# Two stages of a graph network stop loading key rows, and a rare tile is turned on the chip instead

## The reference

```python
src, dst = src[argsort(dst)], sorted(dst)
x = layernorm(x + gnn0(x, src, dst))
x = layernorm(x + gnn1(x, edge_index, edge_attr_32, ...))
x = layernorm(x + attention(x, edge_index, ...))          # needs x[dst] of every edge
s1 = concat(xs[:, :8], xd[:, :8]); v1 = ...               # xs = x[src], xd = x[dst]
edge_out = concat(tanh(scal), vecs * tanh(gates)) * norm
x = layernorm(x + segment_sum(edge_out, dst))             # tensor product
```

## Time and profile before

| | |
|---|---|
| median of 3 runs | 26533.92 us (26527.65 to 26547.35) |
| profiled execution | 26542.53 us, span 26540.7 us |
| busy share of the span | PE 57%, DVE 58%, POOL 59%, ACT 20% |
| attention scatter | about 12034 to 16020 us |
| tensor product | about 18390 to 26500 us |

### The profile page before, as it was taken

One profiled execution on the slowest core, in us unless ns is written; L12 is line 12 of the kernel. 1 busy time (PEld: TensorE's weight loads), 2 busy tenths in 40 slices (PEclk: granted clock), 3 DMA queues, 4 the chain that ended last, 5 costly groups with the idle time before them and its releaser, 6 DMA issues. The chain is left out here.

```text
span 26540.7 us, 456722 instructions
## 1 busy us (share of the span) xinstructions
PE 15258.6 (57%) x102440; PEld 9002.1 (34%) x102441; DVE 15401.4 (58%) x31597; ACT 5213.2 (20%) x13760; POOL 15770.5 (59%) x16798
## 2 busy tenths in 40 slices
PE   7555555566666689951000000024777777787777
PEld 5344444333333388920000000023333333333333
DVE  9666666656566644431111118985666666666666
ACT  4211111111111144410000000000222222222222
POOL 0377777677777744416777777721555555555554
PEclk9655555555555555555555555555888888888888
DMA  2466666433333345403333332212444444444444
GB/s 66 117 173 172 173 173 173 112 68 69 68 69 68 63 148 154 131 15 86 92 92 92 92 92 70 71 46 66 111 111 111 110 110 110 110 111 110 110 110 104
DMA packets 2864906, 2738.33 MB, mean 103 GB/s; under 512 B 1320271, under 2 KB 2226317, under 8 KB 2861906
## 3 DMA queue, kind: packets, MB, share of 16 engines
q1 hardware_dynamic: 2297486, 2308.45, 31.4%
q0 software_dynamic: 412544, 241.53, 6.1%
q10 hardware_dynamic: 153668, 172.93, 2.6%
HBM read 2173.30 MB, written 537.93 MB: 102 GB/s over the span
## 5 line engine op out<-in xcount | busy, mean ns | idle before, releaser
L2225 POOL DMA_INDIRECT rows_x<-x_table,index x3125 | 2974.6, 952 | 3538.4 <-DMA index<-in_src 2765.6
L742 POOL DMA_INDIRECT rows<-split_table,index x3125 | 2999.6, 960 | 1937.5 <-DMA index<-in_src 1008.2
L1624 POOL DMA_INDIRECT rows_dram<-rows,place_now x3125 | 3026.4, 968 | 1484.9 <-issue 952.3
L858 POOL DMA_INDIRECT rows<-x_table,index x3125 | 3279.8, 1050 | 1021.3 <-issue 952.1
L2339 DVE TENSOR_TENSOR second<-banks,h 128x768 f32<-128x768 f32 x2500 | 1944.8, 820 | 1597.8 <-PE banks L2494 1597.8
L1552 DVE TENSOR_REDUCE rows<-banks 128x108 f32<-128x324 f32 x1250 | 490.7, 434 | 3467.3 <-DMA rows_dram<-rows,place_now 3450.7
L1564 PE MATMUL banks<-row_pieces,hot_turned 128*128 x3125 | 394.1, 291 | 3604.6 <-DMA hot_turned<-turned_dram 3602.0
L2331 DVE TENSOR_TENSOR first<-banks,h 128x768 f32<-128x768 f32 x2500 | 1937.9, 818 | 259.3 <-issue 138.3
L550 PE MATMUL banks<-counts,low_turned 128*128 128x98 f32 x6250 | 1793.3, 435 | 80.3 <-ACT counts L538 47.3
L550 PEld LDWEIGHTS banks<-counts,low_turned 128*128 128x128 f32 x6250 | 1600.9, 314 | 205.4 <-issue 175.1
L2469 PE MATMUL banks<-u_turned,w_tensor 32*128 32x384 f32 (+1 forms) x10000 | 1565.0, 501 | 145.3 <-DVE second L2339 145.3
(11 more groups left out here) (480 smaller groups left out, 33841.6 us busy)
## 6 DMA issues: line engine op xcount, KB each, us to landing
key_row<-dst_rows SPq DMA_DIRECT2D x1250, 320.0 KB, 3.5
h<-hidden_dram SPq DMA_DIRECT2D x1250, 320.0 KB, 4.2
acc_moved<-dst_rows SPq DMA_DIRECT2D x625, 320.0 KB
src_row<-in_src_rows SPq DMA_DIRECT2D x625, 320.0 KB
hot_turned<-turned_dram SPq DMA_DIRECT2D x1250, 160.0 KB, 3.2
hot_dram<-onehot SPq DMA_DIRECT2D x625, 160.0 KB
turned_dram<-hot_turned SPq DMA_DIRECT2D x625, 160.0 KB
a_dram<-a ACTq DMA_DIRECT2D x625, 160.0 KB
```

The lines of the kernel that those rows point to most:

```text
L742: nc.gpsimd.indirect_dma_start(out=m["rows"][j][:, t * SPLIT:(t + 1) * SPLIT], out_offset=None, in_=m["split_table"], in_offset=bass.Indir ...
L858: nc.gpsimd.indirect_dma_start(out=m["rows"][j][:, t * C2:t * C2 + F], out_offset=None, in_=m["x_table"], in_offset=bass.IndirectOffsetOnA ...
L1624: nc.gpsimd.indirect_dma_start(out=m["rows_dram"], out_offset=bass.IndirectOffsetOnAxis(ap=m["place_now"][j][:, t:t + 1], axis=0), in_=m[" ...
L2225: nc.gpsimd.indirect_dma_start(out=m["rows_x"][j][:, t * F:(t + 1) * F], out_offset=None, in_=m["x_table"], in_offset=bass.IndirectOffsetO ...
```

## The change

No key row is loaded in these two stages any more. The tables `key_row` and `part_at` go. If a group has a further visit, DVE makes the straight one-hot tile (edges on partitions) from the resident keys, PE turns it by multiplying each of its five 128x128 tiles with an identity matrix, and DVE copies the five results into `turned_more`. In the scatter the keys (128x3125 floats) are loaded once at the start of the stage, DVE and PE wait for that and for the half-precision identity, and `hot_turned` gets five buffers, loaded after `owned` of the group five before instead of after a join. In the tensor product `hot_turned` keeps three buffers; the line that issued `key_row` is gone and the rest of SP's order stands.

```diff
+def turn_spare_dve(nc, dve, m, s, g, further, k, bank):
+    dve.wait_ge(s["more_owned"], ONE + further + k - 1)
+    spare_hot(nc, m, g, k).then_inc(s["spare_hot"], 1)
+    for t in range(T):
+        dve.wait_ge(s["spare_turned"], ONE + T * (further + k - 1) + t + 1)
+        nc.vector.tensor_copy(m["turned_more"][:, t * P:(t + 1) * P], bank).then_inc(s["spare_out"], 1)
+def turn_spare_pe(nc, pe, m, s, further, k, bank):
+    pe.wait_ge(s["spare_hot"], ONE + further + k)
+    for t in range(T):
+        pe.wait_ge(s["spare_out"], ONE + T * (further + k - 1) + t)
+        nc.tensor.matmul(bank, m["hot_spare"][:, t * P:(t + 1) * P], m["ident_half"][:, :], start=True, stop=True).then_inc(s["spare_turned"], 1)
+    pe.wait_ge(s["spare_out"], ONE + T * (further + k))
...
 (stage_attention_tables)
-            link(nc.vector.tensor_scalar(m["part_at"][:, :], m["starts"][:, :], m["part"][:, :], None, ALU.add))
...
 (stage_attention_scatter)
-        dve.wait_ge(s["key_in"][j], 16 * (i + 1))
         with dve.If(n > 1):
             with dve.Fori(1, n) as k:
-                dve.wait_ge(s["more_owned"], ONE + further + k - 1)
-                nc.vector.tensor_scalar(m["turned_more"][:, :], m["key_row"][j % 3][:, :], m["part_at"][:, bass.ds(k, 1)], None, ALU.is_equal
-                                        ).then_inc(s["more_turned"], 1)
+                turn_spare_dve(nc, dve, m, s, SLOTS * i + j, further, k, spare_bank)
...
+            sp.dma_start(m["keys"][:, :], m["keys_dram"]).then_inc(s["loaded"], 16)
             def load(i, j):
                 g = SLOTS * i + j
-                if not (isinstance(i, int) and g < 3):
-                    sp.wait_ge(s["joined"], ONE + g - 1)
-                sp.sem_inc(s["going_sp"], 1)
-                sp.dma_start(m["hot_turned"][j % 3][:, :], ...)
-                sp.dma_start(m["key_row"][j % 3][:, :], key_row_of(m, g, "dst_rows")).then_inc(s["key_in"][j], 16)
+                if not (isinstance(i, int) and i == 0):
+                    sp.wait_ge(s["owned"], ONE + g - SLOTS + 1)
+                sp.dma_start(m["hot_turned"][j][:, :], ...)
...
 (block.tensor)
+            pe.wait_ge(s["halved"], ONE + 1)
 (block.vector)
+            nc.vector.tensor_copy(m["ident_half"][:, :], m["ident"][:, :]).then_inc(s["halved"], 1)
+            dve.wait_ge(s["loaded"], 16)
...
 (stage_directions)
-            link(nc.vector.tensor_scalar(m["part_at"][:, :], m["starts"][:, :], m["part"][:, :], None, ALU.add))
+            link(nc.vector.tensor_copy(m["ident_half"][:, :], m["ident"][:, :]))
...
 (stage_tensor_product, sp_group)
-        sp.dma_start(m["key_row"][j % 3][:, :], key_row_of(m, g, "dst_rows")).then_inc(s["key_in"][j], 16)
 (dve_turned_further)
         with dve.If(n > 1):
             _, visits, further = half_window_of(nc, dve, m, s, SLOTS * i + j)
-            dve.wait_ge(s["key_in"][j], 16 * (i + 1))
-            turned(slice(1, 2)).then_inc(s["more_turned"], 1)
-            with dve.If(visits > 2), dve.Fori(2, visits) as k:
...
+            with dve.Fori(1, visits) as k:
+                turn_spare_dve(nc, dve, m, s, SLOTS * i + j, further, k, spare_bank)
 (pe_own_further)
-                pe.wait_ge(s["more_turned"], ONE + further + k)
-                pe.sem_inc(s["going"], 1)
+                turn_spare_pe(nc, pe, m, s, further, k, spare_bank)
```

More of the change, by code:

```diff
@@ L183, in visits_pe, with spare_hot @@
         product(k, m["onehot_more"])
+def spare_hot(nc, m, g, k):
+    return nc.vector.scalar_tensor_tensor(cut(m["hot_spare"][:, :], t=T), rep(m["keys"][:, bass.ds(T * g, T)], 2, P),
+                                          m["starts"][:, bass.ds(k, 1)], rep(m["ramp"][:, :], 1, T), ALU.subtract, ALU.is_equal)
+def turn_spare_dve(nc, dve, m, s, g, further, k, bank):
[10 more added lines that the diff above has]
+    pe.wait_ge(s["spare_out"], ONE + T * (further + k))
 def halves_sp(sp, m, s, width):
@@ L1563, in own_pe @@
         for t in range(T):
-            mm = nc.tensor.matmul(owned(j, t), m["hot_turned"][j % 3][:, t * P:(t + 1) * P], of_window(first), start=t % 3 == 0, stop=True,
+            mm = nc.tensor.matmul(owned(j, t), m["hot_turned"][j][:, t * P:(t + 1) * P], of_window(first), start=t % 3 == 0, stop=True,
                                   skip_group_check=True)
@@ L2877, in build @@
         with ExitStack() as scope:
-            sb("row_pieces", HALF_WINDOWS * PIECES * XA, BF16, into=scope); sb("part_at", NB, into=scope)
+            sb("row_pieces", HALF_WINDOWS * PIECES * XA, BF16, into=scope);
             with ExitStack() as inner:
@@ L2889, in build @@
                 sb("turned_more", T * P, BF16, into=inner)
-                m["hot_turned"] = [inner.enter_context(nc.sbuf_tensor(f"hot_turned_{nc.next_id()}", [P, T * P], BF16)) for k in range(3)]
-                m["key_row"] = [inner.enter_context(nc.sbuf_tensor(f"key_row_{nc.next_id()}", [P, T * P], F32)) for k in range(3)]
+                m["hot_turned"] = [inner.enter_context(nc.sbuf_tensor(f"hot_turned_{nc.next_id()}", [P, T * P], BF16)) for k in range(SLOTS)]
+                hot_tiles(inner, BF16, 0); sb("hot_spare", T * P, BF16, into=inner); sb("ident_half", P, BF16, into=inner)
                 m["rows"] = [inner.enter_context(nc.sbuf_tensor(f"rows_{nc.next_id()}", [P, T * XA], F32)) for j in range(SLOTS)]
                 m["place_now"] = [inner.enter_context(nc.sbuf_tensor(f"place_now_{nc.next_id()}", [P, T], I32)) for j in range(SLOTS)]
-                stage_attention_scatter(nc, m, sems("att_scatter", "going going_sp going_dve going_pool windows owned joined more_owned more_turned",
-                                                    "turned_in key_in place_now scattered"))
+                stage_attention_scatter(nc, m, sems("att_scatter", "loaded halved going going_dve going_pool windows owned joined more_owned spare_hot spare_turned spare_out",
+                                                    "turned_in place_now scattered"))
         with ExitStack() as inner:
@@ L2920, in build @@
             m["hot_turned"] = [scope.enter_context(nc.sbuf_tensor(f"hot_turned_{nc.next_id()}", [P, T * P], BF16)) for k in range(3)]
-            m["key_row"] = [scope.enter_context(nc.sbuf_tensor(f"key_row_{nc.next_id()}", [P, T * P], F32)) for k in range(3)]
+            sb("hot_spare", T * P, BF16, into=scope); sb("ident_half", P, BF16, into=scope)
             sb("w_tensor", 512, into=scope); sb("w_second", 8 * U8, into=scope); sb("unit_sum", F, into=scope); sb("unit_spread", P, into=scope)
-            sb("x_pieces", HALF_WINDOWS * PIECES * F, BF16, into=scope); sb("part_at", NB, into=scope)
+            sb("x_pieces", HALF_WINDOWS * PIECES * F, BF16, into=scope);
             with ExitStack() as inner:
@@ L2944, in build @@
                 stage_tensor_product(nc, m, sems(
-                    "tp", "piece rest second_piece split first_gained gained halves_in all_added going_sp going_dve joined owned more_owned more_turned step to_root rooted finished stored added_up going going_pool multiplied prepared turned flipped brackets weighted "
+                    "tp", "piece rest second_piece split first_gained gained halves_in all_added going_sp going_dve joined owned more_owned spare_hot spare_turned spare_out step to_root rooted finished stored added_up going going_pool multiplied prepared turned flipped brackets weighted "
                     "unit_sums units_out spread doubled contracted outputs_out returned along vector_parts totalled vectored summed_up bounded gated edge_rows "
-                    "windows first_summed first_added more_hot summed added", "gathered indexed axes_in hidden_in copied key_in hot_in turned_in"))
+                    "windows first_summed first_added more_hot summed added", "gathered indexed axes_in hidden_in copied hot_in turned_in"))
 def by_group(a):
```

8 lines of the change are left out of this document (3 added, 5 removed).

## The result

The kernel after the change takes 26085.88 us (26067.87 to 26103.72) against 26530.78 for the kernel before in the same runs: 0.9832 of it, interval 0.9817 to 0.9847. It is 445 us faster, where the forecast was some 190.

A forecast was written before the change was run, and what follows sets the result against it. The prediction took a latency loop in the tensor product, run about 312 times, as the bound. From the profiled 26542.53 us, less 207, plus 10 and 5, it got 26350.5, lowered to the runs' median and rounded to 26340; range 26090 to 26540.

The forecast's parts named there:

- What bounds the kernel: Tensor product: a latency loop of 25.79 us, run about 312 times, no engine its limit; attention scatter: paced by POOL.
- SP's step: Tensor product: without `key_row` SP issues the index 0.53 us sooner per loop, 207 us gained, ends 165 and 620.
- the row's bytes don't stand in the way: Tensor product: h1 waited for its own issue, not behind key_row's data; had data stood in the way, 1.44 us.
- The slope read from chance variation: Tensor product: over 262 loops, each us of earlier index shortens the loop by 1.25 us, ends 1.0 and 1.38.
- The scatter: Attention scatter: dropping `key_row` gives 0 us; loading keys first makes the first join 5 us later, ends 3.3 and 18.
- further visits: Both branches: no group has a second visit, so what the change adds inside them is skipped and costs nothing.
- Longer code: Tensor product: a tenth more PE program delays the index by 0 to 0.12 us a loop; 10 us, ends 0 and 45.
- the three signs: Forecast wrong if index landing absorbs 0.53 us, PE idles unawaited more than once a round, or slow-turn clock leaves 0.78.
- the forecast case: Whole kernel: the summed terms hold, giving 26340 us, own range 25930 to 26430; chance 0.70.
- Code fetch stalls: PE: the longer skipped block adds a 5.6 us stall per round, 230 us; two more give 26802 us; chance 0.11.
- Nothing comes of it: Tensor product: the index waits behind other data, so SP's earlier step is eaten, 26549 us; chance 0.11.
- The clock stays up: Tensor product: PE's shorter wait keeps it at 2.4 GHz, 905 us more go, 25440 us; chance 0.08.

The follow-up runs named there:

- e4: The changed kernel with the index load of group g+3 issued before SP waits for the gate: 25151.23 us, 0.9477 of the kernel before.
- e7: The kernel before, key row kept, with the index load of group g+3 issued before SP waits for the gate: 25131.65 us, 0.9482 of the kernel before.
- e6: The kernel before without the load of `key_row` in the tensor product, nothing else changed: 26241.04 us, 0.9898 of the kernel before.
- e2: The changed kernel with the 320 KB key row loaded again at its old place in the tensor product, read by nobody: 26223.99 us, 0.9882 of before.
- e15: e2 with 64 matmuls that never run put ahead of PE's tensor product loop: 26769.69 us, 1.0086 of the kernel before.
- e12: The changed kernel with 64 matmuls that never run put ahead of PE's tensor product loop: 26535.14 us, 0.9986 of the kernel before.
- e3: The changed kernel with the 320 KB key row loaded in the tensor product ahead of SP's wait for the gate: 26097.02 us, 0.9833 of before.
- e1: The changed kernel with a 2.5 KB load, read by nobody, where `key_row` stood in the tensor product: 26151.58 us, 0.9857 of the kernel before.
- e8: The kernel before with only the attention scatter's part of the change, the tensor product as it was: 26292.63 us, 0.9919 of the kernel before.
- e5: The kernel before with PE's skipped block in the tensor product made as long as in the changed kernel: 26620.68 us, 1.0042 of before.
- before at its +64: The kernel before with 64 matmuls that never run put ahead of PE's tensor product loop: 26381.60 us, 0.9928 of the kernel before.
- e16: e4 with 64 matmuls that never run put ahead of PE's tensor product loop: 25305.39 us, 0.9536 of the kernel before.

## Why the prediction was wrong

**What bounds the kernel: right.** The latency loop from gate to index to gather sets the stage (e4 and e7 open it and 1400 us go), no engine does, and POOL's pace in the scatter did not move.

**SP's step: right, and its 207 us within what the runs gave.** Axes come 0.53 us sooner as forecast, the index 0.46 in the mean. Taken off alone, the row was worth 1.0% (e6); put back, 0.5% (e2 against after) and 1.0% (e15 against e12), a mean of 0.84% or 223 us. By the fit it is less, since a us of early issue is worth 1.06 per loop and not 1.25: 0.46 x 1.06 x 312 = 152 us. That the row's bytes don't stand in the way holds only in part: moved off the loop they cost nothing (e3), but at the old place they were some 72 us (e2 against e1). The slope read from chance variation in the earlier trace rows could not part an early issue from a short way, and by the fit these have different prices.

**The scatter: right, with some luck in the number.** 5 us were forecast for its start and 5.2 came, but 1.8 of them were there before the stage began; the stage's own 3.3 are the low end that the prediction gave, since the keys landed in 7.0 us where 8.5 was put in. The other parts hold: further visits never ran, and nothing shows on the new helper's lines.

**Longer code: this step failed.** It was the term of +10 us, with ends 0 and 45, reasoned from how many packets are added and from the premise that most packets don't meet an index. Before the change one stood ahead of the index in 268 of 500 groups. What counted is when the packets move. The change lengthens PE's program in the scatter and in the tensor product, so the same 16 KB packets fall elsewhere in the loop. There they mostly no longer stand before the index (23 of 500 groups); its way shrank by 0.52 us, by the fit 0.52 x 1.93 x 312 = 313 us, and the stall by 0.35 us, 15 more. With SP's 152 that makes 480 for 458 measured. So a term of +10 was in truth some -330 by the fit, or -306 as what SP's 152 leaves of the 458; and it could as well have been some +100, for e12 minus after is (0.9986 - 0.9832) = 1.54%, about 410 us, from placement alone. None of the three signs by which the prediction was to be known as wrong looks at the index's way: it had no sign for a shorter one. The time lies 4 us below the range given and inside the forecast case's own, 25930 to 26430. That is no merit: the low end there stood for row data in the way at 620 us, and the runs show some 72.

That it is PE's program is shown by instructions on PE that never run: they move the way between 4.58 and 4.99 us in before and between 4.47 and 5.08 in after. It fits that the kernels with after's program (after, e1, e2, e3) have a way of 4.40 to 4.51 us, with the row or without, and before and e6 4.99 and 4.87; but these two sets differ in DVE's program as well. Over four placements (0, 32, 64, 96) the mean ratio is 0.9954 for before and 0.9898 for after. So the change is worth some 0.56% or 149 us on average. With four values each that spread over 0.7% and 1.5%, this mean difference has a standard error of 0.4%; the row's own 0.84%, taken at equal places, lies within it. Most of the rest of the 1.68% was the luck of its place.

**The rivals.** "Code fetch stalls" named the right resource and the wrong mechanism: PE stalls once a round as before, 41 times, and none of the 625 jumps over the longer block stalled (line view, for the earlier trace rows):

```profile
L2591 PEldq COMPARE_BRANCH  x625: 208/213/229, 18411.4 to 26027.0; - x157
```

"Nothing comes of it" is out, since the row alone brings 1.0% (e6). "The clock stays up" is out: from 18700 to 25000 us the granted clock was 0.87 after and 0.86 before. In the slow turn of the loop shown it rose, from the 0.78 of the earlier trace rows (columns as there):

```profile
22020.00:22033.09 13.09, 10.11 (x83) 4.01 (x84) 9.03 (x20) 3.49 (x10) 8.79 (x11) 0.87 0.37 87
```

The Trainium skill ("Runtime: NRT & Kernel Launch", "Instruction fetch mechanics") says the sequencer fetches the next 16 KiB page through its own DMA queue and that crossing a page's edge is mostly hidden. For PE the trace agrees between round ends: in groups 100 to 599 of the kernel after, PE idles over 3 us nowhere but at the 33 round ends. Of data that move at the same time the section says nothing, and there the cost was not hidden: 0.98 us of straggling against 0.12.

**Open.** In e8 the scatter's edits move the programs of PE, DVE and SP at once; their shares were not parted. In the change itself DVE's program grew too, and no run moves DVE's alone. Why the stall at a round's end takes 5.4 us at one placement and 9.2 at another was not measured; that it hangs on where the loop's first instructions lie within a packet is a guess that no run tests. e5 has before's way and before's issue and is slower by 111 us; the longer stall explains 41 x 1.18 = 48 us of it.

## What to carry to other kernels

A change of a per cent in a long unrolled loop cannot be credited to what it does until the program has been moved, with skipped instructions, to several places and the mean taken, and even four places left a standard error of 0.4% here. A single comparison could have read anything from -1.7% to -0.1% for the same edit, and +0.6% with before at its +64 (0.9986 / 0.9928). When a small load closes a latency loop, issue it ahead of the wait instead of taking things off its path: that gained three times as much as this change, and made the one move of code that was tried cheaper as well (154 us in e16, 410 in e12). In a forecast, a term for longer code needs ends on both sides of nothing.

## What the runs showed of the hardware

PE's instruction packets (16.4 KB, some 1.14 us each by their records) took 0.6% of the time of the 16 DMA engines. Yet with such a packet ahead of it, the last rows of a 2.5 KB load came 0.98 us behind the 120th, and 0.12 us with none; mostly it was exactly eight of 128 rows, which is why I take them to share one engine with the packet. And PE's stall at the end of an unrolled round was 5.3 to 9.6 us in the means of these kernels; 64 instructions that never ran took it from 5.70 to 8.15 in before and from 5.35 to 9.21 in after.
